# A GpSimd memset and a wait behind each row gather of the first buffer fill, in both edge layers of a graph network

## The chip, the cores and the metric

The kernel runs on one core of one Trainium2 chip, in one launch. The metric is the device time in microseconds, the median of three runs. Its engines are TensorE (PE in the profile; PEld are its weight loads), VectorE (DVE), ScalarE (ACT), GpSimd (POOL) and SyncE (SP), which here only issues DMAs.

## What is computed

Four graph layers stand one behind the other, each on the layer-normed and rectified node rows (6250 nodes of 16 values, 206,250 edges sorted by destination) and each added back to the node rows. The first is a graph autoencoder with six graph convolutions and the third a single graph convolution; both run as dense products with an adjacency matrix and are not touched here. The second and the fourth are the two edge layers:

```
...
# second layer: a 16x16 matrix for each of 8 edge types, then a GRU cell
A = edge_emb[edge_type].reshape(-1, MSG_DIM, HID_DIM)
h_src = features[edge_src]
msg = jnp.einsum('emh,eh->em', A, h_src)
m = jax.ops.segment_sum(msg, edge_dst, num_segments=n_nodes)
...
# fourth layer: a 16x16 matrix for each of 90 relations, times a score of the edge
h_src = h[src]
e = jnp.concatenate([z_src, z_e, z_dst], axis=1) @ Wa.T
msg = jnp.einsum('ei,eio->eo', h_src, W_rel[rel_type]) * e
h_out = jax.ops.segment_sum(msg, dst, num_segments=n_nodes)
```

## The kernel before

The edges, padded, are cut into 202 blocks of 1024 (`SUP` = 8 tiles of 128). Each edge layer goes over the blocks in order and has two ways for one:

- **By matmul.** VectorE makes one-hot columns of the source node (`make_hot`), TensorE multiplies them with the node rows (`gather`, L1837 and L2239), ScalarE copies the result (`sel`, L1844 and L2245), TensorE folds it (L1854, L2254), VectorE or TensorE apply the edge type, and TensorE adds up the destinations (L1888 and L1909, or L2326). Keys for the one-hots are loaded by SyncE.
- **By table** (80 blocks in the first edge layer, 96 in the second). A table in HBM holds for every pair of node and type the finished message (16 or 17 float32). GpSimd gathers the block's rows with 8 indirect DMAs of 128 rows each into one row buffer (`fetch_rows`, L1814; `fetch_table_rows`, L2205); later TensorE adds them up (`row_sums`, L1934; `add_up`, L2326).

In the second edge layer the first 11 blocks are a third kind: their node rows are gathered plainly (`fetch_plain_rows`, L2191) while the table is made.

There are `RG` = 8 row buffers in the first edge layer and `RT` = 12 in the second. The gathers of table block g go into buffer g modulo 8 or 12, so GpSimd waits for the sum of block g-8 (g-12) before it issues them, and for nothing but the finished table (and in the second layer, for half of the buffers, the end of the plain blocks) while g is below 8 (12). The engines' order is that of the program's text: in each round i of the layer's loop the matmul block i is gathered, blocks i-1 to i-3 are finished, and the table blocks behind block i are fetched; a table block is summed two or three rounds later. The first table block comes with round 4 of the first edge layer (sum in round 7) and with round 13 of the second (sum in round 15). GpSimd does nothing else in either loop.

`link(pool, ins)` issues an instruction with a semaphore increment and makes the same engine wait for it.

Of the kernel before, what the change touches and what calls it, by code (L numbers as in the profile page):

```python
# [11 lines left out]
P = 128  # L12
# [104 lines left out]
def need(eng, *tokens):  # L117
    for sem, value in tokens:
        eng.wait_ge(sem, value)  # L119


def program(nc, t, wcols, out):
    pe, dve, act, pool, sp = nc.tensor, nc.vector, nc.scalar, nc.gpsimd, nc.sync
    engines = [pe.engine, dve.engine, act.engine, pool.engine, sp.engine]
    life = ExitStack()
# [12 lines left out]
    def step(eng, ins):  # L138

        return done[eng].by(ins)  # L140

    def link(eng, ins):

        tok = step(eng, ins)
        need(eng, tok)
        return tok

    def sb(stack, name, shape, dt=F32):
        return stack.enter_context(nc.sbuf_tensor(name, list(shape), dt))
# [54 lines left out]
    latent_w = sb(life, "latent_w", [32, 32])[:, :]  # L204
    latent_b = sb(life, "latent_b", [32, 1])[:, :]
    growth = sb(life, "growth", [1, 10])

    def w(name):
        if not isinstance(name, str):
            return name  # L210
        r, c0, c1 = wcols[name]
        return W[0:r, c0:c1]
# [1067 lines left out]
    def layers_fast(h_tok):  # L1280
# [418 lines left out]
        def typed_layer(x_spread, HT):  # L1699
# [7 lines left out]
            RG = 8  # L1707
# [98 lines left out]
            def fetch_rows(g):  # L1806
                b, k = g % RG, GK[g]
                if g == 0:
                    pool.wait_ge(*index_ready)
                    pool.wait_ge(s_tab.sem, s_tab.n)  # L1810
                if g >= RG:
                    pool.wait_ge(*a_tok[g - RG])
                for j in range(SUP):
                    r_tok_[g] = r_in[b].by(pool.indirect_dma_start(  # L1814
                        rows[b][:, j, :], None, t1_dram, bass.IndirectOffsetOnAxis(ap=idxA[:, k * SUP + j:k * SUP + j + 1], axis=0)), 16)

            def make_hot(i):
                b = i % 2
                dve.wait_ge(*keys_tok[i])
                if i >= 2:  # L1820
                    dve.wait_ge(*gat[i - 2, HALVES - 1])
                for j in range(GJ - 1):
                    dve.tensor_scalar(hot[b][:, j, :], krow[i % 3][:, :], w("at_key")[:, j:j + 1], None, ALU.is_equal)
                hot_tok[i] = c_hot.by(dve.tensor_scalar(hot[b][:, GJ - 1, 0:HE], klast[i % 3][:, :], w("at_key")[:, GJ - 1:GJ], None, ALU.is_equal))
# [151 lines left out]
            for i in range(n + 3):  # L1976
# [6 lines left out]
                if i < n:  # L1983
                    for g in after[i]:
                        fetch_rows(g)
# [71 lines left out]
        def relation_layer(x_spread, terms, wx, w_ready):  # L2057
# [26 lines left out]
            RG, RT, MC = 6, 12, 2 * F + 1  # L2084
# [109 lines left out]
            def fetch_table_rows(g):  # L2194
                b, k = g % RT, GK[g]
                if g == 0:
                    pool.wait_ge(*index_ready)
                    for m in range(NT - ST, NT):
                        pool.wait_ge(*stored_tok[m])
                if g >= RT:  # L2200
                    pool.wait_ge(*a_tok[GK[g - RT]])
                elif g >= RT - RG:
                    pool.wait_ge(*slot_free[max(r for r in range(PLAIN) if r % RG == g - (RT - RG))])
                for j in range(SUP):
                    rt_tok[g] = r_in[b].by(pool.indirect_dma_start(  # L2205
                        table_rows[b][:, j, 0:RC], None, t3_dram, bass.IndirectOffsetOnAxis(ap=idxA[:, k * SUP + j:k * SUP + j + 1], axis=0)), 16)

            def make_hot(i):
                b = i % 2
                dve.wait_ge(*keys_tok[i])  # L2210
                if by_matmul[i]:
                    if i >= 2 and by_matmul[i - 2]:
                        dve.wait_ge(*gat[i - 2, HALVES - 1])
                    else:
                        for m in range(NT - ST, NT):
                            if m % ST >= 3:
                                dve.wait_ge(*stored_tok[m])
                        dve.wait_ge(*c_x.by(dve.memset(hot[b][:, GJ - 1, :], 0.0)))
                    for j in range(GJ - 1):
                        dve.tensor_scalar(hot[b][:, j, :], krow[b][:, :], w("at_key")[:, j:j + 1], None, ALU.is_equal)  # L2220
                    hot_tok[i] = c_hot.by(dve.tensor_scalar(
                        hot[b][0:ROWS6, GJ - 1, :], klast[b][:, :], w("at_key")[0:ROWS6, GJ - 1:GJ], None, ALU.is_equal))
                if i >= 3:
                    dve.wait_ge(*w_tok[i - 3, SUP // 2 - 1])
                ty_tok[i] = c_ty.by(dve.tensor_scalar(tyh[i % 3][:, :], trow[b][:, :], iotaP[0:R90, :], None, ALU.is_equal))
# [127 lines left out]
            for i in range(n + 2):  # L2353
# [3 lines left out]
                if i < n:  # L2357
                    for g in after[i]:
                        fetch_table_rows(g)
# [43 lines left out]
        ring.append(dinvB[:, 0:NT * CH // 4].bitcast(FP8).rearrange("p (k d) -> p k d", k=NT))  # L2403
        gru_c = gru_constants(tag)
        h_turned = typed_layer(x_spread, gru_c["HT"])
        x_tok, _ = gru_step(tag, m1_dram.rearrange("n s c -> n (s c)"), gru_c, h_turned, load_back)

# [16 lines left out]

        l3 = ExitStack()
        relation_layer(x_spread, terms, wx, w_ready)
        finish(tag, l3, m3_dram.rearrange("n s c -> n (s c)"), [*sums_out, *keys_in])
        return [c.sem for c in (*keys_in, *rows_in, *sums_out)]
# [108 lines left out]
```

## Time and profile before

| | |
|---|---|
| time, median of 3 runs | 4385.97 us (4368.68 to 4389.03) |
| span of the profiled execution | 4363.3 us |
| what lies around the span, against the median | 22.7 us |
| first edge layer, gathers (first to last start) | 1460.2 to 2563.0 us |
| second edge layer, table gathers | 2928.3 to 4242.7 us |
| PE busy | 3616.4 us, 83% |
| DVE busy | 2704.6 us, 62% |
| POOL busy | 1907.4 us, 44% |
| ACT busy | 1310.6 us, 30% |
| mean granted TensorE clock | 0.886 of full speed |

The span runs from the first to the last instruction of one profiled execution; a run's time has what lies around it as well. For a gather the profile shows the time in which GpSimd makes the transfer's descriptors, not the transfer. "Issue" as a releaser means that the engine waited for nothing that the profile shows, "remote" that a semaphore event was the last thing before, with no instruction found for it.

### The profile page before, as it was taken

To read this page: it belongs to the slowest core of one execution; us is meant where nothing else is said; L and a number is where in the kernel's file an instruction comes from. 1 tells how busy PE (TensorE), PEld (TensorE's weight loads), DVE (VectorE), ACT (ScalarE), POOL (GpSimd) and SP (SyncE) were. 2 spreads that over 40 slices of the span, in tenths; PEclk is the share of its full clock that TensorE was granted. 3 is DMA by queue.
4 is the path that set the end of the run, shared out by engine and by line. 5 is a ranking of instruction groups with operands and counts; after the bars stand their busy time and mean duration, and the time that the engine had idled before them with its cause. 6 is when DMAs were issued, how large, how long until landed. Compare 5 with 4: busy or idle time off the path is not lost. (4 is left out here: it accounts for less than half of the span.)

```text
span 4363.3 us, 77744 instructions
## 1 busy us (share of the span) xinstructions
PE 3616.4 (83%) x28548; PEld 2114.8 (48%) x28548; DVE 2704.6 (62%) x6415; ACT 1310.6 (30%) x2874; POOL 1907.4 (44%) x1856
## 2 busy tenths in 40 slices
PE   6787879999998478888888886661899989998888
PEld 4566645544554234444444443330555555555555
DVE  8999953322212356767666674451777767777777
ACT  6999920011000123333233231330222212222222
POOL 1000006830000546777677640357366666666550
PEclk8999989999998689999899897765888888889998
DMA  5444467663366312222222227761222222222221
GB/s 148 83 82 82 66 267 297 218 235 121 151 246 259 88 41 51 51 51 51 47 51 51 51 45 249 271 206 13 41 44 44 44 39 44 44 44 44 39 43 40
DMA packets 471196, 445.62 MB, mean 102 GB/s; under 512 B 357554, under 2 KB 406610, under 8 KB 459676
## 3 DMA queue, kind: packets, MB, share of 16 engines
q1 hardware_dynamic: 389178, 391.82, 29.3%
q0 software_dynamic: 55216, 38.70, 6.4%
q10 hardware_dynamic: 26417, 10.05, 0.9%
q8 instruction: 232, 3.80, 0.4%
q14 instruction: 153, 1.25, 0.1%
HBM read 346.18 MB, written 95.85 MB: 101 GB/s over the span
## 5 line engine op out<-in xcount | busy, mean ns | idle before, releaser
L1814 POOL DMA_INDIRECT rows<-typed_table,ring x640 | 764.1, 1194 | 348.5 <-issue 182.0
L2239 PE MATMUL l_ps_g<-ring,h_part 128*128 128x512 f16 x2660 | 651.1, 405 | 108.4 <-issue 83.8
L1408 PE MATMUL L_ps<-ring,L_T 128*128 128x448 fp8e4 (+1 forms) x4606 | 671.2, 386 | 44.6 <-DMA ring<-adj 41.0
L2205 POOL DMA_INDIRECT ring<-typed_table,l_idxA x384 | 398.5, 1038 | 274.9 <-PE l_ps_x L2326 161.2
L1408 PEld LDWEIGHTS L_ps<-ring,L_T 128*128 128x128 f16 (+1 forms) x4606 | 327.8, 105 | 374.5 <-issue 62.0
L2205 POOL DMA_INDIRECT l_rows<-typed_table,l_idxA x384 | 392.1, 1021 | 252.6 <-PE l_ps_x L2326 146.6
L1875 DVE TENSOR_TENSOR dinvB<-G,tyh 128x1024 f16<-128x1024 f16 x244 | 288.4, 1223 | 337.5 <-ACT G L1862 215.3
L2239 PEld LDWEIGHTS l_ps_g<-ring,h_part 128*128 128x128 f16 x2660 | 275.5, 104 | 453.4 <-issue 190.7
L2245 ACT ACTIVATE l_sel<-l_ps_g 128x512 f16<-128x512 f32 x380 | 226.0, 597 | 855.5 <-PE l_ps_g L2239 375.5
L620 PE MATMUL cells<-keys,lows 128*128 128x147 f16 (+5 forms) x2744 | 372.7, 283 | 121.2 <-DVE keys L581 107.3
L2220 DVE TENSOR_SCALAR ring<-l_krow,W 128x1024 f16<-128x1024 f16 x570 | 234.7, 482 | 304.9 <-remote 178.0
L2274 PE MATMUL l_ps_w<-rel,l_tyh 90*128 90x256 bf16 x2544 | 383.3, 319 | 16.1 <-DVE ring L2302 10.8
L620 PEld LDWEIGHTS cells<-keys,lows 128*128 128x128 f16 x2744 | 286.4, 141 | 204.8 <-DVE keys L581 174.9
L581 DVE TENSOR_SCALAR keys<-build_or_wx,offset 128x441 f16<-128x441 f16 (+3 forms) x1438 | 366.5, 330 | 0.0
L1420 DVE SCALAR_TENSOR_TENSOR L_Y<-L_ps,L_scale,dinvB 128x448 f32<-128x448 f32 x84 | 57.4, 684 | 495.5 <-PE L_ps L1408 495.4
L1837 PE MATMUL ps_g<-ring_fifth,h_part 128*128 128x512 f16 x1464 | 353.4, 401 | 1.5 <-issue 1.4
L1837 PE MATMUL ps_g<-dinvB,h_part 128*128 128x512 f16 x1464 | 351.9, 399 | 1.0 <-issue 0.9
L698 ACT ACTIVATE ring<-cells 128x784 fp8e4<-128x784 f32 x392 | 324.2, 828 | 24.9 <-PE cells L620 24.6
L2274 PEld LDWEIGHTS l_ps_w<-rel,l_tyh 90*128 90x128 bf16 x2544 | 280.9, 113 | 88.6 <-issue 21.7
L1844 ACT ACTIVATE sel<-ps_g 128x512 f16<-128x512 f32 x488 | 263.2, 598 | 186.4 <-PE ps_g L1837 110.9
L2302 DVE TENSOR_TENSOR ring<-l_ps_w,l_G 128x512 f32<-128x512 f32 x380 | 258.4, 682 | 50.2 <-remote 46.5
L2294 DVE TENSOR_REDUCE l_msg<-ring 128x32 f32<-128x512 f32 x424 | 277.7, 676 | 0.0
(369 smaller groups left out, 4415.8 us busy)
## 6 DMA issues: line engine op xcount, KB each, us to landing
ring<-adj SPq DMA_DIRECT2D x67, 2744.0 KB, 10.9
adj<-ring SPq DMA_DIRECT2D x14, 2744.0 KB, 9.2
typed_table<-ring SPq DMA_DIRECT2D x49, 765.0 KB
ring_fifth<-src_div_mod_rows SPq DMA_DIRECT2D x122, 256.0 KB
l_krow<-src_div_mod_rows SPq DMA_DIRECT2D x95, 256.0 KB
l_trow<-type_row SPq DMA_DIRECT2D x106, 180.0 KB
attr<-in_he POOLq DMA_DIRECT2D x25, 512.0 KB, 6.5
klast<-last_keys SPq DMA_DIRECT2D x81, 128.0 KB
```

Of the source, the lines that this page charges most:

```text
L581: ins = dve.tensor_scalar(keys[g % OB][:, j, 0:C], iotaC[:, 0:C], offset[g // BG % 2][:, g % BG, j:j + 1], HIT, ALU.is_equal, ALU.mult)
L620: ins = pe.matmul(to, lows[g // QG % 3][:, :, g % QG * KT + j], made[:, (a1 - a) * NT:(b1 - a) * NT], start=j == FIRST[h], stop=j == LAST[ ...
L698: act.activation(ring[c % RING][:, :, gl * GD:(gl + 1) * GD].rearrange("p k (h d) -> p k h d", h=2), cells[g % CB][:, :, 0:HD * NT].rearra ...
L1408: ins = pe.matmul(bank[at:at + rows, 0:CH], d["T"][q][:, k, 0:rows], ring[r][:, k, :], start=n < side, stop=n >= NT - side, tile_position= ...
L1814: r_tok_[g] = r_in[b].by(pool.indirect_dma_start(rows[b][:, j, :], None, t1_dram, bass.IndirectOffsetOnAxis(ap=idxA[:, k * SUP + j:k * SUP ...
L1837: ins = pe.matmul(ps_g[2 * h + p][:, 0:HE], parts[p][:, j, :], hot[b][:, j, h * HE:(h + 1) * HE], start=False, stop=j == GJ - 2)
L1844: selt[i, h] = c_sel.by(act.activation(sel[b][2 * h + p][:, :], ps_g[2 * h + p][:, 0:HE], ACT.Relu))
L1875: typed_tok[i] = c_typed.by(dve.tensor_tensor(typed[b][:, p, :, :, :], gp, ty, ALU.mult))
L2205: rt_tok[g] = r_in[b].by(pool.indirect_dma_start(table_rows[b][:, j, 0:RC], None, t3_dram, bass.IndirectOffsetOnAxis(ap=idxA[:, k * SUP + ...
L2239: ins = pe.matmul(ps_g[p][:, 0:HE], parts[p][:, j, :], hot[b][:, j, h * HE:(h + 1) * HE], start=j == 0, stop=j == GJ - 1)
L2274: ins = pe.matmul(ps_w[q][:, (j % 2) * 256:(j % 2 + 1) * 256], tyh[i % 3][:, j * P:(j + 1) * P], rel[:, p, :], start=p == 0, stop=p == 2)
L2294: return c_msg.by(dve.tensor_reduce(m[:, 2 * q:2 * q + 2, 0:F], prod[q], AX.X, ALU.add))
```

## The change

A tile `pause` of 128x128 float32 is added. In `fetch_rows` each of the 64 gathers with g below 8, and in `fetch_table_rows` each of the 96 gathers with g below 12, is followed by a memset of the whole tile on GpSimd (128 columns), and GpSimd waits for that memset's completion before it goes on. Nothing reads `pause`. The plain gathers and all later table gathers stay as they are.

```diff
     growth = sb(life, "growth", [1, 10])
+    pause = sb(life, "pause", [P, 128])
...
                 for j in range(SUP):
                     r_tok_[g] = r_in[b].by(pool.indirect_dma_start(
                         rows[b][:, j, :], None, t1_dram, bass.IndirectOffsetOnAxis(ap=idxA[:, k * SUP + j:k * SUP + j + 1], axis=0)), 16)
+                    if g < RG:
+                        link(pool, pool.memset(pause[:, :], 0.0))
...
                 for j in range(SUP):
                     rt_tok[g] = r_in[b].by(pool.indirect_dma_start(
                         table_rows[b][:, j, 0:RC], None, t3_dram, bass.IndirectOffsetOnAxis(ap=idxA[:, k * SUP + j:k * SUP + j + 1], axis=0)), 16)
+                    if g < RT:
+                        link(pool, pool.memset(pause[:, :], 0.0))
```

The lines behind the first edit are one or more lines further down in the changed kernel (L1814 becomes L1815, L2205 becomes L2208). On GpSimd, at the start of the first edge layer, these rows stood in its queue before; a row with x63 is 63 gathers in a row, and the semaphore `pe_types_and_messages` is the sum that frees a buffer:

```order
L1659 DMA dinvB<-h_rows 16x128 x4
L1814 DMA rows<-typed_table,ring 128x16 [waits table_out,index_in]
L1814 DMA rows<-typed_table,ring 128x16 x63
L1814 DMA rows<-typed_table,ring 128x16 [waits pe_types_and_messages]
L1814 DMA rows<-typed_table,ring 128x16 x7
L1814 DMA rows<-typed_table,ring 128x16 [waits pe_types_and_messages]
L1814 DMA rows<-typed_table,ring 128x16 x7
```

Now the same place begins and ends so, with one memset between each two gathers and a wait (`done_pool`) on every gather behind one:

```order
L1660 DMA dinvB<-h_rows 16x128 x4
L1815 DMA rows<-typed_table,ring 128x16 [waits table_out,index_in]
L1818 MEMSET pause 128x128
L1815 DMA rows<-typed_table,ring 128x16 [waits done_pool]
L1818 MEMSET pause 128x128
...
L1818 MEMSET pause 128x128
L1815 DMA rows<-typed_table,ring 128x16 [waits done_pool]
L1818 MEMSET pause 128x128
L1815 DMA rows<-typed_table,ring 128x16 [waits pe_types_and_messages,done_pool]
L1815 DMA rows<-typed_table,ring 128x16 x7
L1815 DMA rows<-typed_table,ring 128x16 [waits pe_types_and_messages]
L1815 DMA rows<-typed_table,ring 128x16 x7
```

What moved is only GpSimd's own order: 64 memsets lie between the first 64 gathers, and the gather that waits for TensorE is the 65th as before. In the second edge layer the fill stood so, where `l3_table_out` and `l3_index_in` are the table and the indices, `dve_products` the end of a plain block and `pe_summed` the sum that frees a buffer:

```order
L2191 DMA l_rows<-h_rows,l_srcA 128x16 [waits dve_products,act_table]
L2191 DMA l_rows<-h_rows,l_srcA 128x16 x7
L2205 DMA ring<-typed_table,l_idxA 128x17 [waits l3_table_out3,l3_table_out4,l3_table_out2,l3_table_out5,l3_table_out1,l3_table_out6,l3_table_out0,l3_index_in]
L2205 DMA ring<-typed_table,l_idxA 128x17 x47
L2205 DMA l_rows<-typed_table,l_idxA 128x17 [waits dve_products]
L2205 DMA l_rows<-typed_table,l_idxA 128x17 x7
...
L2205 DMA l_rows<-typed_table,l_idxA 128x17 x7
L2205 DMA ring<-typed_table,l_idxA 128x17 [waits pe_summed]
L2205 DMA ring<-typed_table,l_idxA 128x17 x7
L2205 DMA ring<-typed_table,l_idxA 128x17 [waits pe_summed]
```

and now its end stands so:

```order
L2211 MEMSET pause 128x128
L2208 DMA l_rows<-typed_table,l_idxA 128x17 [waits done_pool]
L2211 MEMSET pause 128x128
L2208 DMA l_rows<-typed_table,l_idxA 128x17 [waits done_pool]
L2211 MEMSET pause 128x128
L2208 DMA ring<-typed_table,l_idxA 128x17 [waits pe_summed,done_pool]
L2208 DMA ring<-typed_table,l_idxA 128x17 x7
L2208 DMA ring<-typed_table,l_idxA 128x17 [waits pe_summed]
L2208 DMA ring<-typed_table,l_idxA 128x17 x7
```

Here 96 memsets have come in, and the first gather that waits for a freed buffer is the 97th as before. On the other engines no instruction is added, removed or moved.

## Rows read from the trace of the kernel before

**Rows 1.** The page, parts 1 and 2: span, busy tenths in 40 slices.

```profile
span 4363.3 us, 77744 instructions
...
PE   6787879999998478888888886661899989998888
...
POOL 1000006830000546777677640357366666666550
```

**Rows 2.** The waits of 1440 to 2600 us: us in total, times, longest.

```profile
PE ps_x L1854 <- ACT sel L1844: 77.1, 55, 36.7
```

**Rows 3.** Timeline of GpSimd, first fill: start us, us, what, count, idle before.

```profile
1460.20 1.06 POOL L1814 DMA_INDIRECT rows<-typed_table,ring  x1 [8.94 <-DMA typed_table<-dinvB]
...
1543.44 0.95 POOL L1814 DMA_INDIRECT rows<-typed_table,ring  x1 [0.30 <-issue]
1582.71 0.97 POOL L1814 DMA_INDIRECT rows<-typed_table,ring  x1 [38.32 <-PE ps_x L1909]
```

**Rows 4.** Timeline of TensorE behind the start of that fill.

```profile
1512.83 0.19 PE L1909 MATMUL ps_x<-W,dinvB 128*64 128x16 f32 x1 [1.21 <-issue]
1549.69 0.54 PE L1854 MATMUL ps_x<-fold,sel 128*128 128x16 f16 x14 [36.67 <-ACT sel L1844]
```

**Rows 5.** Windows: busy us (instructions) of each engine, TensorE clock, DMA share, GB/s.

```profile
1490.00:1548.00 58.00, 8.09 (x40) 3.56 (x38) 3.51 (x6) 1.58 (x4) 41.29 (x44) 0.57 0.08 6
1582.00:2564.00 982.00, 851.77 (x7777) 449.34 (x7773) 662.19 (x1245) 301.44 (x817) 699.15 (x576) 0.91 0.25 51
1724.00:1886.00 162.00, 145.57 (x1360) 76.82 (x1360) 114.65 (x218) 51.61 (x141) 124.04 (x102) 0.96 0.26 54
2950.00:3060.00 110.00, 15.92 (x52) 5.99 (x51) 7.81 (x17) 2.07 (x4) 76.79 (x81) 0.52 0.12 11
3099.00:4244.00 1145.00, 1036.52 (x8227) 639.54 (x8223) 860.55 (x1973) 249.10 (x575) 696.47 (x672) 0.89 0.24 43
```

**Rows 6.** DMA queues, 1485 to 1550 us: packets, MB, share of 16 engines.

```profile
q0 software_dynamic: 1536, 0.40, 8.0%
```

**Rows 7.** Timeline of ScalarE in the second fill.

```profile
3023.72 0.60 ACT L2245 ACTIVATE l_sel<-l_ps_g 128x512 f16<-128x512 f32 x1 [19.00 <-issue]
```

**Rows 8.** Timeline of GpSimd, the second fill.

```profile
2928.25 1.01 POOL L2205 DMA_INDIRECT ring<-typed_table,l_idxA  x1 [2.63 <-DMA typed_table<-ring]
...
3099.05 1.11 POOL L2205 DMA_INDIRECT ring<-typed_table,l_idxA  x1 [47.76 <-PE l_ps_x L2326]
```

**Rows 9.** Timeline of GpSimd near the start of the program.

```profile
2.09 0.20 POOL L345 MEMSET I<- 128x128 f32 x1
2.45 0.53 POOL L346 TENSOR_SCALAR_AFFINE_SELECT I<-I 128x128 f32<-128x128 f32 x1 [0.16 <-POOL I L345]
...
32.57 2.38 POOL L745 DMA_DIRECT2D m_rows<-zf  x4 [0.31 <-POOL zf L741]
```

**Rows 10.** Timelines of GpSimd and TensorE, 3478 to 3536 us.

```profile
3480.93 1.43 POOL L2205 DMA_INDIRECT ring<-typed_table,l_idxA  x1 [4.09 <-PE l_ps_x L2326]
...
3525.23 0.94 POOL L2205 DMA_INDIRECT l_rows<-typed_table,l_idxA  x1 [0.30 <-issue]
...
3526.64 5.88 PE L2239 MATMUL l_ps_g<-ring,h_part 128*128 128x512 f16 x14 [9.79 <-issue]
```

**Rows 11.** Timelines of GpSimd and TensorE, 1636 to 1680 us.

```profile
1638.70 1.24 POOL L1814 DMA_INDIRECT rows<-typed_table,ring  x1 [6.91 <-PE ps_x L1909]
...
1673.71 0.94 POOL L1814 DMA_INDIRECT rows<-typed_table,ring  x1 [0.30 <-issue]
...
1676.83 0.86 PE L1934 MATMUL ps_x<-rows,dstw 128*64 128x16 f32 x13 [1.11 <-issue]
```

**Rows 12.** Timelines: TensorE at 1581 us, ScalarE from 4255 us.

```profile
1581.68 0.65 PE L1934 MATMUL ps_x<-rows,dstw 128*64 128x16 f32 x16
...
4255.11 0.19 ACT L2337 ACTIVATE l_sums<-l_ps_x 64x32 f32<-64x32 f32 x1 [0.45 <-PE l_ps_x L2326]
...
4266.06 0.19 ACT L2337 ACTIVATE l_sums<-l_ps_x 64x32 f32<-64x32 f32 x1 [0.45 <-PE l_ps_x L2326]
```

## The prediction

> **What bounds the kernel now.** I read first the page's slices, 109 us each [rows 1]. TensorE is the fullest engine nearly everywhere, at 8 or 9 tenths, and so bounds most of the span. It has two holes: 4 tenths in the 14th slice (1418 to 1527 us) and 1 tenth in the 28th (2945 to 3054 us). Both lie at the start of an edge layer, where GpSimd begins its row gathers. The change sits there, and the rest of the span only moves as a block.
>
> Next, the waits of the first edge layer [rows 2]: one of TensorE's for a ScalarE copy lasts 36.7 us, of 77.1 in 55. Such a copy takes 0.60 us in the second layer [rows 7], so something held ScalarE. The timelines show what else went on. GpSimd issues its first 64 gathers (8 buffers of 8) from 1460.2 to 1544.4 with nothing between them but the 0.30 us that it always leaves [rows 3]: 84 us, 1.32 us each, and 1.25 us each (0.94 busy and 0.30) once VectorE has fallen silent. TensorE crawls, one small matmul and then 1.2 us without one, with the releaser "issue", stops at 1513, and is back at 1549.7 [rows 4], some 5 us behind the last gather. In the stretch 1490 to 1548 TensorE is busy 8.1 us of 58, VectorE 3.5, ScalarE 1.6, GpSimd 41.3 [rows 5]. The releasers are "issue" and "remote", no late operand; and transfers are no bottleneck, since the gathers' own packets fill 8% of the DMA engines in that time [rows 6].
>
> The second edge layer shows the same, longer. Its 96 gathers (12 buffers of 8) run from 2928.3 to 3051.3 (3099.05 less 47.76), 1.28 us each [rows 8], and between 2950 and 3060 TensorE is busy 15.9 us of 110 [rows 5]; a 0.60 us copy of ScalarE starts 19.0 us behind the one before it [rows 7]. I take it that a long unbroken series of gathers starves the issue of all other engines, by whatever path, until the series ends. What is lost: 58 less the work done in it, about 52 us in the first layer, and about 95 of 110 in the second.
>
> **From which series length on.** Later GpSimd is held by freed buffers, and it issues 576 gathers in 982 us (1.70 us each) and 672 in 1145 (1.70 each), with TensorE busy 87 to 91% [rows 5]. So 1.7 us each is borne. Series that are denser are not: in the first layer 24 gathers in a row at 1.50 us each (1638.7 to 1674.7) leave gaps of 1.1 us in TensorE at their end [rows 11]. In the second, 32 gathers from 3480.9 to 3526.2 (1.42 us each) end with TensorE idle for 9.8 us, and it is back 0.5 us behind the last of them [rows 10]. Trouble thus starts after some 24 gathers at 1.25 to 1.5 us, and lasts as long as the series does.
>
> **The change, part by part.** Added are 64 and 96 memsets of 128x128 float32 with a wait for each one's semaphore. The only memset of that form in the trace takes 0.20 us, and the instruction that waits for it starts 0.16 us behind its end; a DMA behind a memset starts 0.31 us behind it [rows 9]. No row has a memset behind a gather: it could start at once or after the usual 0.30 us. An interval is thus 0.94 + (0 to 0.30) + 0.20 + (0.31 to 0.46) = 1.45 to 1.90 us with VectorE silent. Beside a working VectorE the gathers are longer: 699.15/576 = 1.21 us busy in the first layer, 696.47/672 = 1.04 in the second [rows 5]. With 0.20 for the memset and 0.4 for both gaps, nearer the low end since the wait may overlap the usual gap, I take 1.8 us for the first layer and 1.65 for the second.
>
> Here the Trainium skill has something to say, on the page SBUF — State Buffer, section "SBUF: two separate sides": GpSimd cannot write its descriptors while VectorE holds the shared port. By it the gathers are longer beside VectorE's work, and the trace agrees (1.21 against 0.94 us); it changes no term, since I use the durations as they stand.
>
> The fills then end at 1460 + 64 x 1.8 = 1575 and at 2928 + 96 x 1.65 = 3086. GpSimd's queue behind a waiting memset holds only gathers, and the first user of them comes late: the first row sum is at 1581.7, after eight rounds [rows 12], so with the stall gone still at about 1530, when three to four buffers are full (15 us each). The (1.8 - 1.32) x 64 = 31 and (1.65 - 1.28) x 96 = 35 us that the memsets cost GpSimd are covered by that lead; without the cover they would fall on TensorE in full.
>
> By themselves, spacings of 1.65 to 1.8 lie at or above what is borne, so the stalls of 52 and 95 us go. But **what is late next** is GpSimd. While it fills slowly, TensorE runs on and frees buffers. When the memsets stop, all of these are open at once, and the gathers run unbroken again, now without a memset between.
>
> First layer: TensorE frees its first buffer at about 1531 instead of 1582.7 (the 52 us), then one each 12.8 us (a little below the 982/72 = 13.6 of before [rows 5]). At 1575 some 4.4 buffers are free (35 gathers). The series starts with 24 gathers at 1.5 us (36 us, 2.8 more buffers free); of 7.2 x 8 = 58 gathers 34 are left, which run at 1.25 us with TensorE starved: 42 us and 4 behind them. That ends at 1657 with 7.2 buffers used. Before, the same stood at 1582.7 + 6.2 x 13.6 = 1667. Gain 10 us.
>
> Second layer: the first free buffer at 3099 - 95 = 3004 [rows 8]. A round, and with it a buffer, takes 10.95 us undisturbed [rows 12] and 1145/84 = 13.6 beside gathers [rows 5]; I take 12.5. At 3086 there are 1 + 82/12.5 = 7.6 free. 24 gathers at 1.28 (31 us, 2.5 buffers more), then 10.1 x 8 - 24 = 57 at 1.25, 71 us and 5 behind: end 3193. Before, 3099 + 9.1 x 13.6 = 3223. Gain 30 us.
>
> Sum: 40 us less. The profiled execution spans 4363.3 us [rows 1], which gives 4323; around the span the median of the runs (4385.97) has 22.7 us more, so I say 4346. Ends: nothing given back by the later series makes the gain 50 + 95 = 145 us (4241); full give-back makes it 0.
>
> **Rivals.**
> - *The burst does not come back* (4241 to 4300). TensorE's pace and GpSimd's may interleave well enough. For it: from 1724 to 1886 GpSimd issues 102 gathers in 162 us (1.59 each) while TensorE is 90% busy [rows 5]. Against it: the 9.8 us of [rows 10], where the series was only 32 long. If half of the give-back is missing, 4290.
> - *Same.* The slow fill only moves the stall, in full, behind the fill: GpSimd starts its free running at 1575 and 3086 against 1582.7 and 3099.1 before, nearly the same points. If GpSimd then sets the pace as it does now, the gain is 8 + 13 = 21 us, 4365, inside 0.5%. To it belongs the case that unprofiled runs do not have the stall; against that speaks that the median is 22.7 us above the span and not far below it.
> - *Slower.* The spacing does not matter, only that GpSimd is issuing: then other engines are starved through the longer fills, and the time is 4386 + 31 + 35 = 4452. It decides if the borne spacing lies above 1.8 us. Against it: 1.70 us is borne for a thousand microseconds [rows 5]. A milder form, a spacing of only 1.45 to 1.5 in the second fill, starves it for about 70 gathers x 1.5 = 105 us there (95 now), to which a later series adds some 30: 4386 + 10 + 30 - 10 = 4416.
> - *The gathers are not what starves the engines.* Then only the memsets count, hidden in GpSimd's lead: 4386. The Trainium skill, page SBUF — State Buffer, section "Who interferes with whom", says that a DMA never contends with a compute engine. The stalls' ends 0.5 and 5 us behind the last gather of a series [rows 3, 4, 10] speak against this rival, and so against the rule's use here.
>
> **How the numbers follow.** Chances: the forecast with part of the stall given back (4320 to 4363) 0.44, the burst not coming back 0.19, no difference (both cases) 0.25, slower 0.12. A measurement of this kernel tells about 0.5% (22 us) from nothing: the three runs lie 20 us apart. Faster by more than that 0.63, within it 0.25, slower 0.12. The likeliest time is 4346 with its own range 4320 to 4363; the range for 8 in 10 goes down to where nearly all of the burst stays away and up over the cases without a difference, which leaves out the slow ones (0.12) and less than 0.1 below: 4255 to 4400.
>
> **What would show it.** In the changed profile: memsets of about 0.2 us between the gathers and an interval of 1.6 to 1.9 us; fills ending near 1575 and 3040 to 3090; TensorE above 80% busy from 1490 to 1548 and the first row sum near 1530. Then a series of 50 to 90 gathers without a wait behind each fill, and in it a TensorE stall of about 45 us (first layer) and 80 us (second). If those late stalls are absent, the gain is far larger than I say, and my step on what is late next was wrong. If TensorE still starves between the memsets, the borne spacing was wrong, and the time is at or above that of before.

## The result and the profile after

The changed kernel takes 4314.86 us (median of 16 runs, 4279.19 to 4350.49), the kernel before, measured again beside it, 4372.55 (16 runs, 4328.31 to 4389.03): 57.7 us less by the medians, ratio 0.9875, 95% interval 0.9847 to 0.9903. The ratios here leave out the few runs that lie more than 1.5% above the fastest of their kernel, and are not quite the quotients of the medians. The direction and the wide range (4255 to 4400) held; the gain is larger than the 40 us of the forecast, and the time lies just below the forecast's own range (4320 to 4363). The profiled execution spans 4295.0 us, 68.3 below that of [rows 1]:

```profile
span 4295.0 us, 77912 instructions
...
PE   6787879999999686888888896679639989998998
...
POOL 1000006830000386776676750258756666666650
PEclk8999989998999897998898997769869889888989
```

The 14th slice, 4 before, is 6, and the 28th, 1 before, is 9. New holes lie behind them: a 6 in the 16th (8 before), and 6 and 3 in the 29th and 30th (8 and 9 before). The timeline of GpSimd at the end of the first fill shows how the memsets stand between the gathers:

```profile
1565.18 0.95 POOL L1815 DMA_INDIRECT rows<-typed_table,ring  x1 [0.27 <-POOL pause L1818]
1566.13 0.22 POOL L1818 MEMSET pause<- 128x128 f32 x1
1566.62 0.95 POOL L1815 DMA_INDIRECT rows<-typed_table,ring  x1 [0.27 <-issue]
1567.58 0.22 POOL L1818 MEMSET pause<- 128x128 f32 x1
1568.07 1.81 POOL L1815 DMA_INDIRECT rows<-typed_table,ring  x1 [0.27 <-issue]
```

A memset starts as its gather ends, and the next gather 0.27 us behind the memset (0.30 behind a gather): 1.44 us at the least, and 1.69 on average, (1568.07 - 1459.89)/64, since many gathers, and some memsets, are longer while VectorE works. The windows, to be held against [rows 5]:

```profile
1490.00:1548.00 58.00, 55.94 (x545) 30.39 (x545) 50.29 (x91) 22.19 (x58) 49.02 (x68) 1.00 0.29 62
1600.00:1640.00 40.00, 6.88 (x16) 1.74 (x17) 0.00 (x0) 0.00 (x0) 30.24 (x33) 0.57 0.12 17
2920.00:3060.00 140.00, 138.15 (x1228) 89.22 (x1227) 134.90 (x303) 38.10 (x86) 115.64 (x169) 1.00 0.26 54
3100.00:3180.00 80.00, 11.81 (x29) 3.11 (x30) 0.00 (x0) 0.19 (x1) 56.09 (x60) 0.50 0.10 7
```

TensorE is busy 55.94 of the 58 us where it had 8.09, and 138.15 of 140 us in the second fill, at the full clock. Then, with the memsets gone, comes the stall that the forecast calls late next: 6.88 us of 40, and 11.81 of 80, and VectorE not at all. GpSimd's timeline shows the ends of both series and its waits for TensorE behind them, and TensorE's shows it crawl and come back with the series' end:

```profile
1641.02 0.94 POOL L1815 DMA_INDIRECT rows<-typed_table,ring  x1 [0.30 <-issue]
1651.27 1.87 POOL L1815 DMA_INDIRECT rows<-typed_table,ring  x1 [9.31 <-PE ps_x L1912]
...
3173.14 0.95 POOL L2208 DMA_INDIRECT l_rows<-typed_table,l_idxA  x1 [0.30 <-issue]
3194.20 0.98 POOL L2208 DMA_INDIRECT l_rows<-typed_table,l_idxA  x1 [20.11 <-PE l_ps_x L2331]
```

```profile
1517.70 0.64 PE L1937 MATMUL ps_x<-rows,dstw 128*64 128x16 f32 x16
...
1641.00 0.21 PE L1891 MATMUL ps_x<-dsth,dinvB 128*128 128x64 f16 x1 [2.59 <-issue]
1643.80 0.21 PE L1891 MATMUL ps_x<-dsth,dinvB 128*128 128x64 f16 x1 [2.59 <-issue]
1645.90 0.21 PE L1891 MATMUL ps_x<-dsth,dinvB 128*128 128x64 f16 x1 [1.89 <-issue]
1647.30 0.21 PE L1891 MATMUL ps_x<-dsth,dinvB 128*128 128x64 f16 x1 [1.19 <-issue]
1648.00 0.21 PE L1891 MATMUL ps_x<-dsth,dinvB 128*128 128x64 f16 x1 [0.49 <-issue]
1648.70 0.21 PE L1891 MATMUL ps_x<-dsth,dinvB 128*128 128x64 f16 x1 [0.49 <-issue]
1649.40 0.43 PE L1891 MATMUL ps_x<-dsth,dinvB 128*128 128x64 f16 x5 [0.49 <-issue]
1649.75 1.04 PE L1937 MATMUL ps_x<-rows,dstw 128*64 128x16 f32 x16
```

The gaps before a matmul, 2.59 us each while gathers are issued, shrink to nothing within 8 us behind the last gather (1641.02 + 0.94).

### The profile page after: what moved, and what is told of

Its sections match the earlier page's. It is cut to its first block and busy times, and to the rows that moved or that the text cites. A ratio compares the mean times of both kernels' runs of the same rounds, so it can differ in the third digit from the quotient of the medians.

```text
span 4295.0 us, 77912 instructions
## 1 busy us (share of the span) xinstructions
PE 3623.0 (84%) x28548; PEld 2123.6 (49%) x28548; DVE 2714.1 (63%) x6415; ACT 1312.5 (31%) x2874; POOL 1957.3 (46%) x2016
## 3 DMA queue, kind: packets, MB, share of 16 engines
q14 instruction: 153, 1.25, 0.1%
## 5 line engine op out<-in xcount | busy, mean ns | idle before, releaser
L1815 POOL DMA_INDIRECT rows<-typed_table,ring x640 | 764.0, 1194 | 313.8 <-issue 170.2
L2208 POOL DMA_INDIRECT l_rows<-typed_table,l_idxA x384 | 396.7, 1033 | 230.6 <-PE l_ps_x L2331 123.8
L2208 POOL DMA_INDIRECT ring<-typed_table,l_idxA x384 | 400.0, 1042 | 220.7 <-PE l_ps_x L2331 112.4
L2307 DVE TENSOR_TENSOR ring<-l_ps_w,l_G 128x512 f32<-128x512 f32 x380 | 258.0, 681 | 12.8 <-remote 10.5
```

What stands on the lines that cost most here:

```text
L1815: r_tok_[g] = r_in[b].by(pool.indirect_dma_start(rows[b][:, j, :], None, t1_dram, bass.IndirectOffsetOnAxis(ap=idxA[:, k * SUP + j:k * SUP ...
L2208: rt_tok[g] = r_in[b].by(pool.indirect_dma_start(table_rows[b][:, j, 0:RC], None, t3_dram, bass.IndirectOffsetOnAxis(ap=idxA[:, k * SUP + ...
```

## The experiments

All kernels compute the full result. They ran in five sessions, each on one chip, and the chips are of two kinds, which nothing in the first two profiles told: in the second and fourth session (one and the same chip) the kernel before takes 4370.55 and 4446.63 us, like the 4372.55 above; in the first, third and fifth (three other chips) it takes 3834.43, 3829.41 and 3832.13. I name them chips with and without stalls. Ratios are to the kernel before in the same session, with 95% intervals.

```
                                     with stalls                        without stalls
memsets in both fills (the change)   0.9869 [0.9823, 0.9915] r2_after   1.0183 [1.0157, 1.0209] u1_after
in the first layer's fill alone      0.9940 [0.9901, 0.9979] t1         1.0005 [0.9982, 1.0029] s1, 1.0017 [0.9999, 1.0034] e1
in the second layer's fill alone     0.9959 [0.9925, 0.9993] t2         1.0184 [1.0149, 1.0219] s2, 1.0171 [1.0144, 1.0197] e2
both fills, one column               0.9861 [0.9803, 0.9919] r3
both fills, two memsets a gather                                        1.0242 [1.0209, 1.0275] s3
both fills, then every second        0.9716 [0.9669, 0.9762] t4         1.0387 [1.0353, 1.0420] s4, 1.0314 [1.0291, 1.0337] u2
behind every gather                                                     1.0712 [1.0682, 1.0743] e4, 1.0717 [1.0692, 1.0743] u3
no memset, fetches tied to rounds    1.0068 [1.0024, 1.0113] r4         1.0083 [1.0054, 1.0112] e5
the kernel before itself             1.0025 [0.9988, 1.0062] r1
```

**One layer alone.** The edit takes one of the two memsets out of the change; for the first layer alone:

```diff
                         table_rows[b][:, j, 0:RC], None, t3_dram, bass.IndirectOffsetOnAxis(ap=idxA[:, k * SUP + j:k * SUP + j + 1], axis=0)), 16)
-                    if g < RT:
-                        link(pool, pool.memset(pause[:, :], 0.0))
```

Expected in the first session:

> Memsets and waits only behind the 64 gathers of the first edge layer; the second layer is as before. Theory (a dense series of gathers starves the other engines; the slow fill removes the first stall and a later dense series brings part of it back): faster than before by the first layer's share, 25 us or so of the 58 (ratio 0.994), with a late stall of about 45 us near 1600 us. Rival (the gain comes from the second layer alone): ratio 1.000. Rival (the first layer's stall would be wholly saved): 50 us, 0.988.

> Memsets and waits only behind the 96 gathers of the second edge layer; the first layer is as before, with its stall from 1490 to 1549 us. Theory: faster than before by about 35 to 40 us (ratio 0.991), with a late stall of some 90 us in place of the 105. Rival (both layers' gains hang together, through the state in which the second begins): less than half of it.

In the third and the fourth session:

> Memsets in the first edge layer alone, on a chip that needs about 4370 us for the kernel before. In two pairs of traces the 80th selection copy of ScalarE in the first layer came 26 and 36 us earlier with the memsets, and the layer ended 25 and 57 us earlier. Theory (each layer's stall is replaced by a later and shorter one, and the layers add up): ratio 0.993 (0.989 to 0.996). Rival 1 (what the first layer gains is given back in the second): 1.000. Rival 2 (the first layer brings it all): 0.987. On a chip that needs about 3834 us and has no stalls: 1.00 to 1.002.

> Memsets in the second edge layer alone, on a chip that needs about 4370 us for the kernel before. Reckoned from the layer's start, the 76th selection copy came 24 and 33 us earlier in the two pairs of traces, and the layer's end 40 and 3 us earlier. Theory: ratio 0.994 (0.990 to 0.997), so that the two layers alone add up to the 0.987 of both. Rival (all of the second layer's gain is given back by the later stall): 1.000. On a chip of about 3834 us without stalls: 1.017, since GpSimd sets the pace there.

> The same kernel once more, memsets in the first edge layer alone, for a chip that needs about 4370 us for the kernel before. Theory (the layers add up; each early stall is replaced by a later and shorter one): ratio 0.993 (0.989 to 0.996). Rival 1 (given back in the second layer): 1.000. Rival 2 (the first layer brings all): 0.987. On a chip of about 3830 us without stalls: 1.001, as measured twice.

> The same kernel once more, memsets in the second edge layer alone, for a chip of about 4370 us. Theory: ratio 0.994 (0.990 to 0.997). Rival (the second layer's later stall gives all back): 1.000. On a chip of about 3830 us without stalls: 1.018, as measured twice.

On the chip with stalls the layers bring 0.60% (27 us of 4447, interval 9 to 44) and 0.41% (18 us, 3 to 33); together 0.990, which with these intervals agrees with the 0.987 of both. Each memset works only where it stands, as the windows of the two kernels show (t1 first, then t2):

```profile
1490.00:1548.00 58.00, 55.93 (x555) 30.59 (x553) 50.34 (x91) 22.26 (x57) 49.03 (x67) 1.00 0.26 62
3000.00:3060.00 60.00, 2.97 (x7) 0.87 (x7) 4.53 (x8) 0.60 (x1) 45.37 (x49) 0.53 0.08 7
```

```profile
1490.00:1548.00 58.00, 7.32 (x23) 2.31 (x23) 0.71 (x1) 1.19 (x3) 38.01 (x41) 0.51 0.06 6
3052.00:3171.00 119.00, 116.39 (x1016) 74.22 (x1013) 112.52 (x254) 30.76 (x71) 98.57 (x140) 0.99 0.23 54
3200.00:3260.00 60.00, 10.52 (x22) 2.38 (x23) 0.58 (x2) 0.47 (x2) 45.37 (x49) 0.50 0.09 7
```

The first has TensorE busy in the first fill and starved in the second, the other the reverse, with its late stall at 3200 to 3260.

**The chips without stalls.** The changed kernel was run in the second session and, beside two kernels of a later paragraph, in the fifth:

> The kernel before, profiled on the chip of this call. The four runs before this one took place where the kernel before needs 3834 us and not 4373, and their traces hold no stall at all, with GpSimd issuing 640 gathers without one wait. Theory A (a dense series of gathers starves the other engines only on some chips, or in some condition of a chip): the time is either near 4370 with the stalls at 1490 and 2950 us, or near 3834 without any. Theory B (the stalls come and go between executions on one chip): times between the two, or both in one call.

> The changed kernel beside it. Where the stalls exist: 0.985 to 0.99 of before. Where they do not: GpSimd's series is unbroken from the first gather to the last, so the time that 160 memsets and waits cost it (64 x 0.3 = 20 and 96 x 0.4 = 38 us) falls on the whole: 1.015 to 1.02, as the second layer alone gave 1.017.

> The changed kernel itself, beside the next two on one chip. On a chip with stalls: 0.987 of the kernel before, as in two calls (0.9875 and 0.9869); if the medians of before wander (4370 and 4447 on the same chip in two calls), the share may be larger. Without stalls: about 1.02, the two layers' 1.001 and 1.018 together.

In no session do runs of the kernel before mix the two kinds (at most 94 us between its fastest and slowest run in one session, where the kinds lie more than 470 apart), so the stalls belong to a chip or its condition and not to single executions, as the first theory has it. The second session repeats the result (0.9869). In the fifth the same kernel is slower, 1.0183, and the single layers, measured on two other such chips, put all of that on the second layer (s2 1.0184, s1 1.0005). The windows of the changed kernel there, first fill and behind the second, and of GpSimd's timeline a piece inside the last:

```profile
1460.00:1548.00 88.00, 83.06 (x787) 44.28 (x785) 75.47 (x137) 32.76 (x85) 74.13 (x103) 1.00 0.22 52
3085.00:3110.00 25.00, 24.12 (x209) 14.61 (x207) 22.56 (x53) 6.72 (x16) 19.82 (x18) 1.00 0.22 49
```

```profile
3091.05 0.94 POOL L2208 DMA_INDIRECT ring<-typed_table,l_idxA  x1 [0.30 <-issue]
3092.30 0.94 POOL L2208 DMA_INDIRECT ring<-typed_table,l_idxA  x1 [0.30 <-issue]
3093.55 0.94 POOL L2208 DMA_INDIRECT ring<-typed_table,l_idxA  x1 [0.30 <-issue]
3094.80 0.94 POOL L2208 DMA_INDIRECT ring<-typed_table,l_idxA  x1 [0.30 <-issue]
```

And the first fill of s2, whose first layer is that of the kernel before:

```profile
1460.00:1548.00 88.00, 82.42 (x718) 42.22 (x715) 67.34 (x132) 30.73 (x77) 70.65 (x57) 0.97 0.24 56
```

Eighteen gathers in 25 us, some of them 1.25 us apart, leave TensorE busy 24.12 of 25 us there, and the unchanged first fill leaves it 82.42 of 88. On these chips nothing is starved, and GpSimd never waits for a freed buffer (in the e1 trace all 640 gathers follow each other from 1459.3 to 2478.2), so a pause in it is paid wherever TensorE has no lead of filled buffers left. In the second layer more than the pause is paid: 3900.35 less 3831.86 us (s2, s1) is 68 us, where 96 pauses of 0.19 us (0.22 + 0.27 - 0.30) make 18. The traces put the rest in two places. The fill itself takes 165 us in s2 and 135 in s1, 30 more, since the gathers in it (1.16 against 1.10 us) and some of the memsets (0.28 us on average) are longer too. Behind the fill, without memsets in either, the 672 other gathers take 971 us in s2 and 939 in s1; the idle time between them is the same 204 us in both, but the gathers themselves add up to 767 us against 736. The windows of s1 show first its second fill, and then the same stretch in s1 and in s2:

```profile
2736.00:2871.00 135.00, 135.00 (x1161) 86.32 (x1160) 132.06 (x302) 35.81 (x80) 105.78 (x96) 0.97 0.29 56
2995.00:3445.00 450.00, 450.00 (x4120) 293.49 (x4119) 430.75 (x989) 125.41 (x289) 350.35 (x328) 1.00 0.30 55
```

```profile
2995.00:3445.00 450.00, 429.49 (x3804) 269.23 (x3803) 396.72 (x912) 115.57 (x267) 355.51 (x311) 0.98 0.27 51
```

In s1 TensorE is full here and a gather takes 1.07 us; in s2 it is no longer full and a gather takes 1.14. In s2 VectorE waits for gathered rows in this stretch (49.9 us in 34 waits) and in s1 never: I read this as GpSimd's lead used up by the memsets. Why a gather is longer once the lead is gone was not found. In the first layer the fill is only 8 us longer with the memsets (109 against 101, s1 and s2) and the rest no longer (903 against 908).

**How long a pause.** One column instead of 128; two memsets instead of one:

```diff
-                        link(pool, pool.memset(pause[:, :], 0.0))
+                        link(pool, pool.memset(pause[:, 0:1], 0.0))
```

```diff
                         link(pool, pool.memset(pause[:, :], 0.0))
+                        link(pool, pool.memset(pause[:, :], 0.0))
```

> Memsets of one column in place of 128, waits as in the changed kernel. Theory (the interval counts): about 0.1 us shorter, some 1.35 us each. Where there are stalls: this is too dense, the fills starve TensorE again and the gain shrinks to less than half (0.995 to 1.00). Where there are none: 1.01 to 1.015. Rival (the wait breaks the series whatever its length): as the changed kernel.

> Two memsets behind each gather of the first fills. Interval 0.95 + 2 x (0.22 + 0.27) = 1.93 us with VectorE silent, so fills of 64 x 1.93 = 124 us and 96 x 1.93 = 185 us, ending 15 and 25 us later than with one. No early stall either way. Theory (GpSimd's deficit is worked off in an unbroken series, during which TensorE is starved): about one and two buffers more are open when the memsets stop, so the later stalls are some 10 and 20 us longer and ratio is 0.993 (0.989 to 0.998) on a chip of about 4370 us. Rival 1 (any spacing above what is borne gives the same): 0.987. Rival 2 (the early spacing of 1.67 us still cost something): 0.980. On a chip of about 3834 us: 1.02 to 1.03.

One column does as well by its ratio (0.9861), the number of the rival and not the 0.995 to 1.00 that I expected. But its four runs lie at 4287.6, 4288.7, 4328.3 and 4355.4, and the trace is of the last, so what it shows holds for that execution alone. In it the timeline of GpSimd and the window show the early stall back in the first fill, in spite of the memset and its wait:

```profile
1511.00 0.95 POOL L1815 DMA_INDIRECT rows<-typed_table,ring  x1 [0.27 <-POOL pause L1818]
1511.95 0.11 POOL L1818 MEMSET pause<- 128x1 f32 x1
1512.33 0.95 POOL L1815 DMA_INDIRECT rows<-typed_table,ring  x1 [0.27 <-POOL pause L1818]
```

```profile
1490.00:1548.00 58.00, 11.04 (x39) 2.74 (x40) 6.04 (x11) 2.67 (x6) 45.01 (x84) 0.51 0.06 6
```

The interval is 1.33 us with VectorE silent, against 1.44 with the full tile: in this execution TensorE starved at 1.33, and with the full tile it did not in any of four traced fills of the first layer (the changed kernel twice, t1, t4). So a wait behind each gather is not enough by itself. That the spacing is what helps fits this, and fits the last kernel below, which has no memset and spaces the first fill at 1.84 us; but one trace, of the slowest of four runs, does not show that the 0.11 us decide. Two memsets met only a chip without stalls (1.0242); the interval is 1.70 us at the least, and 1.86 and 1.90 on average in the two fills, where I expected 1.93 at the least, since a memset starts 0.05 us behind another. Whether a longer pause gains where stalls are stays open.

**Behind the fills too.** A memset behind every second gather after the fill, or behind all gathers:

```diff
-                    if g < RG:
+                    if g < RG or j % 2:
```

> As the change, and behind the first fill a memset behind every second gather to the end of each layer. With VectorE silent the interval is then (1.25 + 1.45) / 2 = 1.35 us, beside a working VectorE about 1.6. Theory (a series at 1.35 us starves TensorE as one at 1.25 does, as the first fill with the one-column memset showed): the later stalls stay, and GpSimd needs some 8 per cent more time in the rest, which its waits of 10 us and less between fetches hide; ratio 0.987 (0.983 to 0.995). Rival 1 (the series need to be wholly unbroken to starve the others): later stalls gone, ratio 0.970. Rival 2 (GpSimd becomes the bound): above 1.00. On a chip of about 3834 us without stalls: 1.04.

> As the change, and behind the first fill a memset behind every second gather to the end of each layer, once more for a chip of about 4370 us. Theory: later stalls stay, since a starved series at 1.35 us an interval starves as one at 1.25 does; 0.987 (0.983 to 0.995). Rival 1 (a series must be wholly unbroken to starve the others): later stalls gone, 0.970. Rival 2 (GpSimd becomes the bound): above 1.00. On a chip of about 3830 us without stalls: 1.039, as measured.

> The kernel that measured 0.9716 in the fourth call, where the changed kernel itself was not run beside it. Its profiled execution still had both later stalls (38.8 and 73.4 us of TensorE's idle against 49.0 and 88.0 in the changed kernel's), so Theory 1 says that its lead lies in the long stretches behind them, where the memsets keep the series of gathers looser: 1.0 to 1.8 per cent below the changed kernel, 0.970 to 0.977 of before. Theory 2 (the kernel before happened to be slow in that call, and the two memset kernels are alike): equal to the changed kernel within 0.4 per cent. Without stalls: 1.04.

> The memset and the wait stand behind every gather of both tables, 640 and 768, not only of the first fill. Theory: no dense series is left, so neither the early nor the late stall is there and TensorE never starves; but GpSimd now needs 1.7 us or more for each gather, 640 x 1.75 = 1120 us against the 1087 from the first to the last now, and 768 x 1.65 = 1270 against 1273, so it sets the pace of both layers: 4290 to 4380, ratio 0.98 to 1.00. Rival (only the fill matters and GpSimd has room later): the two late stalls of 45 and 90 us are saved on top, about 4190.

> A memset behind every gather of both layers, on a chip with stalls. There is then no denser series at all. Theory (a series looser than 1.6 us starves nobody): no later stall, and GpSimd sets the pace with 1.69 us each in the first layer (640 in 1082 us, as the changed kernel took 1071 to 1087) and 1.67 in the second (768 in 1283 us, as the changed kernel took 1272 to 1302): equal to the changed kernel within 0.7 per cent. Rival (beside a working VectorE an interval is longer, 1.8 us, and GpSimd is the bound): 1.02 to 1.03 of before. Without stalls: 1.071, as measured.

On the chip with stalls every second gather gave 0.9716, beyond my range and at the number of the first rival. But that rival's mechanism isn't there: the late stall, which it says would be gone, is still in the trace:

```profile
3120.00:3180.00 60.00, 14.32 (x54) 6.29 (x52) 6.89 (x15) 2.07 (x4) 47.19 (x67) 0.53 0.08 7
```

In the first layer the late stall is there too (27.91 of 70 us from 1640 to 1710). Its gain over t1 and t2 lies partly in the long stretches. Between the starts of the 128th and the last gather of the first layer it takes 901 us, t1 917 and t2 942; between the 208th and 768th of the second 936, against 969 in both. The changed kernel itself was not in that session. In the second session, on the same chip, its stretches take 867 and 971 us, those of the kernel before 887 and 941, and its median is 4309.53 us, where this kernel's is 4309.78. So how much of the 0.9716 is the kernel's, and how much that of a session in which the kernel before was 76 us slower on the same chip, is not settled. The two runs that were to settle it (u2, and u3 with memsets behind all gathers) met a chip without stalls. There this kernel costs 3 to 4%, and memsets behind all gathers 7%; what the latter does with stalls was never measured.

**No memset, but no burst either.** Here GpSimd issues the fetches that are due in a round only once TensorE is two or three rounds away, so that buffers are not filled in one series; in the first layer, and likewise in the second with i - 2:

```diff
                     for g in after[i]:
+                        if i >= 3:
+                            pool.wait_ge(*gat[i - 3, HALVES - 1])
                         fetch_rows(g)
```

> No memset at all, the kernel before with another brake: GpSimd may issue a table block's gathers of round i only once TensorE has finished the one-hot matmuls of round i-3 (first edge layer) or i-2 (second), so that it is never more than three or two rounds ahead of its place in the program. Theory: a series is then at most some 24 gathers long, both the early and the late stall are gone, and the two layers lose 52 + 95 us against before: about 4230, ratio 0.966. If the lead is too short for the gathers to land, TensorE waits for rows and the gain is smaller. Rival (the memsets themselves, or their synchronisation, are what helps): no gain over before, ratio 1.00.

> No memset; GpSimd may issue a round's gathers only once TensorE is at most 3 (2) rounds behind. Where there are stalls: the early and the late ones are gone, 0.966 (0.95 to 0.98). Where there are none: 1.008 as in the first call, since GpSimd sets the pace and now starts its series late.

This was my candidate for a better kernel, and it failed with stalls (1.0068) as without (1.0083). The windows of r4, fill and what follows:

```profile
1490.00:1548.00 58.00, 44.98 (x365) 22.53 (x366) 31.86 (x61) 14.36 (x40) 33.53 (x32) 0.83 0.16 40
1660.00:2500.00 840.00, 703.25 (x5893) 360.85 (x5892) 502.45 (x949) 228.04 (x624) 485.43 (x439) 0.84 0.19 45
```

The waits of TensorE at its column sums between 1700 and 2500 us, in the kernel before (r1) and in this one:

```profile
PE ps_x L1888 <- issue: 15.6, 22, 1.2
```

```profile
PE ps_x L1888 <- issue: 71.4, 112, 1.5
```

The long early stall is gone, 44.98 of 58 us where the kernel before has 9.42 in the r1 trace of the same chip. But fetches now come as two at a time, 16 gathers close together, again and again, and TensorE is held at its column sums 112 times where it was 22, always shortly. The granted clock of the long stretch (1660 to 2500 us) is 0.84 against 0.91 in r1, and 5893 matmuls are in it against 6637. I read this as a stall that was spread and not removed; that each hold belongs to a group of gathers was not counted.

## Why the prediction was off in size

**The bound and the two holes** were read rightly, and on chips with stalls the stall hangs on GpSimd's gathers: space them and it goes, in the layer where they are spaced and not in the other (t1, t2). That a long unbroken series of gathers starves the issue of all other engines is true of chips with stalls only. The Trainium skill, page SBUF — State Buffer, section "Who interferes with whom", says that a DMA never contends with a compute engine; where the kernel before takes 4370 us the traces speak against its use here (6.88 us of 40), on the chips where it takes 3830 they agree with it (135.00 of 135 in the second fill of s1). My "some 24 gathers at 1.25 to 1.5 us" is no rule of the program: on a chip without stalls 96 gathers at 1.41 us leave TensorE full.

**The interval.** Forecast 1.8 and 1.65 us, measured 1.69 and 1.67. The memset has no gap before it and 0.27 us behind it, just under my lowest sum of the two (0.31).

**What is late next** came as forecast. First layer: a series of 56 gathers to 1642 (forecast 58, to 1653). Second: 88 gathers behind the fill, to 3174 (forecast 81, to 3188). Both with TensorE starved throughout their later part. The rival in which the burst does not come back fell, and the slower ones too where stalls are. On the other chips the change is slower, by a way that I had priced only in passing: the cover is gone. I had 31 and 35 us for it; it is near 0 in the first layer and some 68 in the second.

**The step that failed** is the first layer's term: "TensorE frees its first buffer at about 1531 instead of 1582.7 (the 52 us), then one each 12.8 us". Both halves of it were too small. The first row sum is at 1517.70, 64 us before the 1581.68 of [rows 12]. The windows up to it show how (the kernel before at 1460 to 1490, 1548 to 1581 and as a whole, then the changed kernel at 1460 to 1490 and as a whole):

```profile
1460.00:1490.00 30.00, 23.43 (x151) 10.20 (x149) 16.50 (x35) 7.07 (x14) 23.71 (x21) 0.83 0.21 45
1548.00:1581.00 33.00, 28.72 (x230) 14.33 (x231) 23.76 (x46) 10.83 (x28) 0.00 (x0) 0.88 0.20 50
1460.00:1581.00 121.00, 60.24 (x419) 28.09 (x418) 43.77 (x85) 19.48 (x46) 65.00 (x64) 0.72 0.14 28
```

```profile
1460.00:1490.00 30.00, 26.44 (x210) 12.79 (x209) 21.93 (x42) 9.79 (x22) 25.10 (x37) 0.97 0.18 42
1460.00:1517.00 57.00, 51.97 (x419) 25.93 (x418) 45.12 (x84) 19.36 (x46) 48.02 (x67) 0.98 0.22 53
```

The same 419 matmuls take 121 us and 57. The stretch from 1490 to 1548 cost about the 52 us that I had, but the kernel before was already some 8 us late at 1490 (151 matmuls against 210) and lost some 3 more behind 1548, at a granted clock of 0.88. And the sixth is at 1569.15, so 10.3 us apiece: with the stall gone TensorE runs at a granted clock of 1.00 and without the small holes of the later stretch (0.91) from which I took the pace. Seven buffers were free at 1590 and not at 1608, so the late series found TensorE further on. The eighth buffer came free at 1651.27, where my working has 1657 + 0.8 x 13.6 = 1668; before, it was at 1678. Put into my working, the measured first sum and pace turn its gain of 10 us into 20, the measured end of the fill (1568 and not 1575) alone into 15, and both into 25; the trace has 27. That near match is in part luck: the working then needs nine buffers for the series where the trace has seven, since the row sums slow to 20 us apiece once the memsets stop (1569.15 to 1589.49). (At 1530 some 4.9 buffers of 14.4 us would have been full by my interval and not three to four; nothing hung on that.) These are the starts of the gather that waits for the eighth buffer, and of two gathers near the end of the second layer's series, less the start of the layer's first gather, in the traces with stalls of the kernel before, of the changed kernel and of its single layers:

```
first layer, 121st gather    without memsets 218.0 (before), 233.9 (r1), 238.7 (t2)   with 191.4 (after), 193.3 (r2), 193.6 (t1)
second layer, 185th gather   without memsets 320.4 (before), 329.9 (r1), 334.5 (t1)   with 292.4 (after), 277.1 (r2), 294.9 (t2)
second layer, 193rd gather   without memsets 335.0 (before), 342.1 (r1), 349.2 (t1)   with 305.0 (after), 308.4 (r2), 309.6 (t2)
```

The first layer gained 27 us there in the first pair of traces, and 41 and 45 in the others, where I had 10; the second, at the 193rd gather, 30, 34 and 40, where I had 30. (At the 185th r2 seems to gain 53, but its series runs on to the 192nd, so that gather has not waited yet.) In the first pair the 121st and the 185th gather make 26.6 + 28.0 = 54.6 of the 68.3 us; the rest, 13.7, came behind, where the time wanders. Between the 185th gather and the end the two kernels take 1114.6 and 1100.8 us in the first pair, and 1100.2 and 1152.5 in the second. By the ratios of whole runs (t1, t2) the split is 27 and 18 us, with intervals of 9 to 44 and 3 to 33, so the runs confirm that both layers count, not which is larger, and the 10 us that I had for the first lies inside its interval: that its term was the one too small rests on the traces.

## What to carry to other kernels

Before a wait is costed from one trace, see that the stall is the program's and not the chip's: the same change was worth 1.3% where stalls are and cost 1.8% on a chip without, and its second half alone cost as much on two more. Here the part that is safe on both is the first layer's (0.994, and 1.0005 to 1.0017), which costs nothing without stalls. When a stall is removed by slowing its cause, take the pace of the waiting engine from the clean stretch that it will now have, at that stretch's clock, and reckon where the debt is paid: here it was, from 20 to 30 us behind the fill on.

## What the runs showed of the hardware

- Chips of one type differ by 14 to 16% on this kernel (3830 against 4370 to 4447 us). In the traces of e1 (first layer's memsets, which cost nothing there) and r1 TensorE is busy 3404 us at a clock of 0.94 against 3634 at 0.884, and idle 438 us against 739. One chip moved by 76 us between two sessions.
- On chips with stalls the average gather of the long stretch takes 1.21 us (699.15/576, [rows 5]) and one beside a silent VectorE 0.94, so a series gets denser once VectorE is starved, and the others stay starved until it ends. That this holds the stall up is my reading and was not tested; a working VectorE alone does not lengthen every gather (four of 0.94 us in u1, in a window with VectorE busy 22.56 of 25).
- On GpSimd a 128x128 memset takes 0.22 us, one column 0.11; the gather behind it starts after 0.27 us and a memset behind a memset after 0.05 (s3). Why some chips starve the other engines during such a series and others don't was not found.
